# Two passes instead of three for the column scores of an attention loop, the shift row's transfer on two DMA queues, and another order of a turn

## The chip, the core and the metric

The kernel runs on one core of one Trainium2 chip. The metric is the device time of one launch, in microseconds, lower is better. The core has five engines that run side by side, each with its own instruction stream in order: TensorE (PE), VectorE (DVE), ScalarE (ACT), GpSimd (POOL) and SyncE (SP). They are kept in step by semaphores. DMAs are issued here by SP and by ScalarE, each on a queue of its own.

## The reference

A small language model's layer on 32 sequences of 128 tokens: token embedding with a windowed feature, one attention block with 16 heads, and a gated mixture of 16 experts. What the change touches is the attention:

```python
q = einsum('bsd,dhk->bshk', x, Wq) + bq
k = einsum('bsd,dhk->bshk', x, Wk) + bk
v = einsum('bsd,dhk->bshk', x, Wv) + bv
scores = einsum('bqhk,bshk->bhqs', q, k) * scale      # scale = 1/sqrt(64)
attn = softmax(scores, axis=-1)
ctx = einsum('bqhk,bshk->bqhk', attn, v)
attn_out = einsum('bqhk,hkd->bqd', ctx, Wo) + bo
y = layernorm(x + attn_out) * gamma + beta
```

The vocabulary has only 28 entries, so every token is a short vector: a one-hot of 28, a windowed share of 28, and a few constant columns, 64 with padding (UD). Two normalisations turn into two factors per token, r1 and r2. The scores of a head are then u^T G u with a 64x64 matrix G per head.

## The kernel before

Three stages stand one behind the other. Stage 1 (the first 46 us) builds tables. Its `nb` holds the token vectors without the factors, 128 tokens on the partitions, `uf` the vectors times r12 = r1 r2. TensorE transposes `uf`, split in two float16 parts, into `ub[r, b, part, :]`: the vectors on 64 rows, tokens along the columns, in both halves of the partitions. `nk` is the float16 copy of `nb` that the values use, with the factors s1 and s12 in its last columns. `keep_going` issues matmuls whose result nobody uses.

Stage 2 is a loop over the 32 sequences, software-pipelined: turn i of the loop handles the scores of sequence i+4, its second half's row scores, the column scores of i+3 and i+2, the values of i+2 and i+1, the output of i+1 and the normalisation of i, all interleaved. Each engine has its own loop over i in STEPS and its own order, written out by hand. The chain for one sequence b, in halves hf of eight heads (names are the functions of the listing below):

- `q_rows` (TensorE) makes G u for four pairs of heads in bank A[hf]; `q_hi` (ScalarE) and `q_lo` (VectorE) split it in float16 parts `qh` and `ql`.
- `score_rows` (TensorE) computes rough scores with queries on the partitions; it writes both banks of A, so it waits for both `q_lo`. `maxima` (VectorE) takes the row maxima, `maxima_cols` (TensorE) transposes them, `max_row` (ScalarE) copies them negated to `mrow`, and SP moves this row by DMA into row SHIFT of `qh` in either half of the partitions, so that the next matmul subtracts the maximum on its own.
- `score_cols` (TensorE) computes the exact scores with keys on the partitions in the two banks ST, as three passes of 512 columns for each 64-row half: high part of u with `qh`, high with `ql`, low part with `qh`. The two halves of the partitions run side by side.
- `exps` and `probs_hi` (ScalarE) take the exponential and its float16 part, `probs_lo` (GpSimd) the rest. `exps(b, 2)` and `exps(b, 3)` read the banks ST that `score_cols(b+1, 0)` writes next, which waits for them; `exps(b, 0)` and `exps(b, 1)` stand the same way before `score_cols(b, 1)`.
- `values` and `turn` (TensorE), `sums`, `sum_root`, `context`, `context_lo` (VectorE) and `context_hi` (ScalarE) make the normalised context, `output` and `residual` (TensorE) the attention's output, `y_squares` (ScalarE), `var_y`, `root_y` (GpSimd) and `y_scaled` (VectorE) its normalisation; `h2`, `var_x`, `x_rows`, `x_cols`, `x_hi`, `x_lo` and `logits` prepare stage 3.

In the first turns, `token_rows` on ScalarE and VectorE fill the residual stream, and `log_rho` (VectorE) with two small exponentials on ScalarE prepares the bias of `exps`. Stage 3 (from about 345 us) is the mixture of experts and isn't touched.

The order of a turn before, on TensorE: residual(i), turn(i+1,0), values(i+1,1), logits(i-1), q_rows(i+4,0), score_cols(i+2,1), maxima_cols(i+3), turn(i+1,1), q_rows(i+4,1), output(i+1,0), values(i+2,0), score_rows(i+4,0), score_cols(i+3,0), x_cols(i), output(i+1,1), score_rows(i+4,1). A row of the trace names the line; in stage 2 these are L1212 `q_rows`, L1225 `score_rows`, L1238 `score_cols`, L1255 `values`, L1264 `turn`, L1273 `output`, L1278 `residual`, L1287 `x_cols`, L1309 `maxima_cols`; on ScalarE L944 `q_hi`, L953 `exps`, L959 `probs_hi`, L965 `context_hi`, L972 `max_row`; on VectorE L1053 `q_lo`, L1062 `maxima`, L1087 `context`, L1096 `context_lo`, L1103 `y_scaled`; on SP L836, the shift.

## Time and profile before

| | us |
|---|---|
| median of three runs | 538.77 (538.43 to 546.91) |
| the profiled execution | 537.01 |
| its span in the trace | 535.2 |
| TensorE busy | 497.3 (93%) |
| VectorE busy | 447.9 (84%) |
| GpSimd busy | 384.7 (72%) |
| ScalarE busy | 379.2 (71%) |
| granted TensorE clock, mean | 0.989 |

Busy means that an instruction of the engine was under way; issuing a DMA, waiting for a semaphore and branching don't count. "Idle before" is the time in which an engine did nothing before an instruction, with the instruction or DMA that ended it. The durations of matmuls overlap, as they are pipelined: the price of a group of matmuls is the distance from its start to the next group's start. ACTq and SPq are issues of DMAs on these engines' queues.

### The profile page before, as it was taken

What the parts mean: (1) busy time and instruction counts of PE and PEld (TensorE: products, weight loads), DVE (VectorE), ACT (ScalarE), POOL (GpSimd) and SP (SyncE); (2) the same over time, 40 slices, a digit from 0 to 9 for tenths busy, and PEclk for the clock granted to TensorE, in tenths of its full rate; (3) what the DMA queues carried; (4) which work ended last, traced back from release to release, by engine and by line L of the source; (5) the groups of instructions that cost most, each with busy time, mean ns of one, the idle gap of its engine ahead of it and who ended that gap; (6) DMA issues with size and microseconds to landing.
All of it is one profiled execution on the core that took longest, in us unless ns stands there. A gap on an engine that the chain in (4) does not pass through costs nothing. (4 is left out here: it accounts for less than half of the span.)

```text
span 535.2 us, 15239 instructions
## 1 busy us (share of the span) xinstructions
PE 497.3 (93%) x5567; PEld 362.8 (68%) x5567; DVE 447.9 (84%) x1054; ACT 379.2 (71%) x768; POOL 384.7 (72%) x519
## 2 busy tenths in 40 slices
PE   5988799999999999999999998769999999999984
PEld 3876567777777777776777775534466767777664
DVE  4797669999999999998999999868778898878675
ACT  2868778888898888988898887336766555556530
POOL 1025669888788888888888888750468798789783
PEclk9998989999999999999999999999999999999998
DMA  6800000000000000000000000000734163351011
GB/s 233 333 6 2 2 2 4 2 3 3 3 2 3 3 3 3 4 2 4 3 4 2 3 3 2 2 1 4 168 80 100 23 150 76 77 138 38 31 40 60
DMA packets 11902, 21.68 MB, mean 41 GB/s; under 512 B 4668, under 2 KB 9780, under 8 KB 10164
## 3 DMA queue, kind: packets, MB, share of 16 engines
q1 hardware_dynamic: 11410, 20.15, 13.8%
q8 instruction: 45, 0.74, 0.6%
q10 hardware_dynamic: 418, 0.55, 0.4%
q14 instruction: 29, 0.24, 0.2%
HBM read 16.24 MB, written 4.33 MB: 38 GB/s over the span
## 5 line engine op out<-in xcount | busy, mean ns | idle before, releaser
L845 POOL TENSOR_TENSOR s_pl<-s_pf,s_ph 128x512 f16<-128x512 f32 x128 | 147.0, 1160 | 8.7 <-ACT s_ph L959 8.7
L1062 DVE TENSOR_REDUCE s_mx<-ps 128x4 f32<-128x512 f32 x128 | 83.8, 677 | 17.6 <-PE ps L1225 14.1
L953 ACT ACTIVATE s_pf<-ps,s_ln_r 128x512 f32<-128x512 f32 x128 | 87.1, 683 | 11.4 <-PE ps L1238 8.9
L823 PE MATMUL ps<-s_xt_all,s_w1s 128*128 128x512 f16 x384 | 87.9, 379 | 2.2 <-ACT s_ub L1543 1.6
L1698 PE MATMUL ps<-s_w2s,s_hid 128*128 128x256 f16 x768 | 88.9, 273 | 0.0
L1698 PEld LDWEIGHTS ps<-s_w2s,s_hid 128*128 128x128 f16 x768 | 75.1, 98 | 11.0
L959 ACT ACTIVATE s_ph<-s_pf 128x512 f16<-128x512 f32 x128 | 74.0, 637 | 0.0
L1273 PE MATMUL ps<-s_zh,s_cth 128*128 128x256 f16 x256 | 69.9, 273 | 1.0 <-DVE s_ctl L1096 1.0
L1273 PE MATMUL ps<-s_zl,s_cth 128*128 128x256 f16 x256 | 69.8, 273 | 0.0
L1273 PE MATMUL ps<-s_zh,s_ctl 128*128 128x256 f16 x256 | 69.8, 273 | 0.0
L823 PEld LDWEIGHTS ps<-s_xt_all,s_w1s 128*128 128x128 f16 x384 | 37.3, 98 | 41.4 <-ACT s_ub L1543 2.1
L1238 PE MATMUL ps<-s_qh,s_ub 64*128 64x512 f16 x256 | 49.5, 383 | 1.1 <-DMA s_qh<-s_mrow 1.1
L1053 DVE SCALAR_TENSOR_TENSOR s_ql<-ps,s_qh 128x512 f16<-128x512 f32 x64 | 43.4, 679 | 7.4 <-ACT s_qh L944 7.1
L944 ACT ACTIVATE s_qh<-ps 128x512 f16<-128x512 f32 x64 | 38.2, 598 | 13.7 <-PE ps L1212 12.1
L1506 POOL TENSOR_TENSOR s_hid<-s_ub,s_hid 128x512 f16<-128x512 f32 x21 | 25.9, 1253 | 27.8 <-ACT s_hid L1550 27.6
L1096 DVE TENSOR_TENSOR s_ctl<-ps,s_cth 128x512 f16<-128x512 f32 x64 | 43.6, 681 | 0.1
L1087 DVE TENSOR_TENSOR s_cn<-ps,s_rsum 128x480 f32<-128x480 f32 x64 | 41.8, 653 | 1.2
L1212 PE MATMUL ps<-s_ub,s_gp 128*128 128x128 f16 x512 | 40.1, 224 | 1.7 <-PEq L218 1.6
L1264 PE MATMUL ps<-s_ident,s_cn 128*128 128x128 f32 x256 | 38.7, 273 | 2.4 <-DVE s_cn L1087 2.4
L965 ACT ACTIVATE s_cth<-ps 128x512 f16<-128x512 f32 x64 | 38.5, 602 | 2.7 <-PE ps L1264 2.7
L1255 PE MATMUL ps<-s_uh,s_ph 128*128 128x60 f16 x512 | 36.8, 190 | 0.2 <-issue 0.2
L1255 PEld LDWEIGHTS ps<-s_uh,s_ph 128*128 128x128 f16 x512 | 32.3, 97 | 6.9 <-issue 6.7
(246 smaller groups left out, 1149.0 us busy)
## 6 DMA issues: line engine op xcount, KB each, us to landing
s_rep<-picks SPq DMA_DIRECT2D x14, 512.0 KB, 6.7
s_stage<-in_w SPq DMA_DIRECT2D x2, 1024.0 KB, 14.3
out<-s_zh SPq DMA_DIRECT2D x16, 128.0 KB, 2.0
out<-s_lg SPq DMA_DIRECT2D x16, 128.0 KB, 1.7
s_stage<-in_wq SPq DMA_DIRECT2D x1, 1024.0 KB, 5.0
s_stage<-in_wk SPq DMA_DIRECT2D x1, 1024.0 KB, 6.7
s_stage<-in_wv SPq DMA_DIRECT2D x1, 1024.0 KB, 8.3
s_stage<-in_wo SPq DMA_DIRECT2D x1, 1024.0 KB, 10.8
```

Source lines behind the costliest of these rows:

```text
L823: mm = nc.tensor.matmul(hidden_bank(n)[:], w1s[:, wp, c, j * P:(j + 1) * P], xt_all[:, GB * g:GB * (g + 1), xp, c, :], start=(k == 0), sto ...
L845: nc.gpsimd.tensor_tensor(flat(pl[:, b % 2, 4 * j:4 * j + 4, :]), pf[:, j, :], flat(ph[:, b % 2, 4 * j:4 * j + 4, :]), ALU.subtract).then_ ...
L953: nc.scalar.activation(pf[:, j, :], ST[j % 2][:], ACT.Exp, bias=ln_r[:, b:b + 1]).then_inc(exp_done[j], 1)
L959: nc.scalar.activation(flat(ph[:, b % 2, 4 * j:4 * j + 4, :]), pf[:, j, :], ACT.Copy).then_inc(phi_done[j], 1)
L1053: nc.vector.scalar_tensor_tensor(out=flat(ql[:, b % 2, hf]), in0=A[hf][:], scalar=1.0 / G_SCALE, in1=flat(qh[:, b % 2, hf]), op0=ALU.mult, ...
L1062: nc.vector.tensor_reduce(mx[:, b % 2, c:c + 4], A[ab][:].rearrange("p (h k) -> p h k", h=4), AX.X, ALU.max).then_inc(max_done[hf][ab], 1)
L1087: nc.vector.tensor_tensor(cn[:, hf].rearrange("p t (a u) -> p (t a) u", u=UD)[:, :, 0:UV], CB[hf][:].rearrange("p (h u) -> p h u", u=UD)[: ...
L1096: nc.vector.tensor_tensor(flat(ctl[:, b % 2, 4 * hf:4 * hf + 4, :]), CB[hf][:], flat(cth[:, b % 2, 4 * hf:4 * hf + 4, :]), ALU.subtract).t ...
L1238: mm = nc.tensor.matmul(ST[ab][:], ub[r, b, part, :], flat(q[r, b % 2, hf]), start=(n == 0), stop=(n == 2))
L1255: mm = nc.tensor.matmul(CB[hf][:, c:c + UV], p[:, b % 2, h, :], nk[:, b, 0:UV], start=(n == 0), stop=(n == 1))
L1273: nc.tensor.matmul(YB[:, 0:D], c[:, b % 2, p, :], zz[:, p, :], start=(p == 0 and c is cth and zz is zh), stop=False)
L1698: mm = nc.tensor.matmul(zb[b % 4], hid[:, g % 2, hp, j, t * P:(t + 1) * P], w2s[:, wp, j, :], start=False, stop=(j == NJ - 1 and hp == 1))
```

## The change

Three things are done at once.

**Two passes.** The column scores no longer use `ub` (u times r12, two float16 parts) but `nkT`, the transposed token vectors without the factors, which need one float16 part. The passes are `nkT` with `qh` and `nkT` with `ql`. The factor r12 of the key comes in as the per-partition scale of the exponential. The factors of the constant rows (R2, ONE, SHIFT, each now two rows for a high and a low part) are written into `nkT` by DMA: `scale_rows` (TensorE) transposes four columns of `nk`, VectorE copies them to `srow`, and SP issues twelve row DMAs. `nkT` itself is made in stage 1: eight groups of eight matmuls on TensorE (some in place of filler), four copies on ScalarE, four on VectorE; ScalarE's copy from `nb` to `nk` stands later. `nkT` takes the memory of `ul`.

**The shift on two queues.** SHIFT has two rows in each half of the partitions, so the maxima's row goes out in four DMAs instead of two: two from SP for the lower half as before, two from ScalarE (`shift_rows`) for the upper half, behind `max_row` and `q_hi(i+4,0)` in ScalarE's order.

**The order of a turn.** TensorE: `score_rows(.,1)` moves from the end of a turn to behind the next turn's `residual`; `maxima_cols` ahead of `score_cols(i+2,1)`; `q_rows(.,1)` ahead of `turn(.,1)`. VectorE: both `q_lo` together at the top, `y_scaled` and the logits earlier, the first half's two maxima exchanged, `log_rho` earlier in the first turns. ScalarE: `probs_hi(.,0)` and `probs_hi(.,1)` from the end of a turn to the beginning of the next, around `context_hi(.,0)`; `max_row` ahead of `q_hi(.,0)`.

The diff, cut to its core:

```diff
-R2, ONE, SHIFT = 2 * V, 2 * V + 1, 2 * V + 2
-ONE_HI, UV = R2 + 2, R2 + 4
+R2, ONE, SHIFT = 2 * V, 2 * V + 2, 2 * V + 4
+UV = ONE + 2
...
-        u_top, u_rest, nk = uh[:, 0], ul[:, 0], uh[:, 1]
+        u_top, nk = uh[:, 0], uh[:, 1]
+        nkT = ul[:].rearrange("p a b u -> p (a b u)").rearrange("p (b t) -> p b t", t=P)
...
+                def nkt_cols(n):
+                    dve.wait_ge(nt_ready, 8 + n + 1)
+                    nc.vector.tensor_copy(nkT[:, 16 + 4 * n:20 + 4 * n, :].rearrange("p b t -> p (b t)"), NKT_BANKS[4 + n][:])\
+                        .then_inc(nkt_ok, 1)
+
+                nkt_cols(0)
+                nkt_cols(1)
...
+                def nkt_part(n):
+                    if 1 <= n < 4:
+                        pe.wait_ge(nt_ok, (1, 2, 4)[n - 1])
+                    elif n >= 4:
+                        pe.wait_ge(nt_ok, 4 + (2, 3, 1, 4)[n - 4])
+                    for k in range(4):
+                        for ab in range(2):
+                            mm = nc.tensor.matmul(NKT_BANKS[n][ab * UD:(ab + 1) * UD, k * P:(k + 1) * P], nb[:, 4 * n + k, :], ident16[:],
+                                                  start=True, stop=True)
+                    mm.then_inc(nt_ready, 1)
+
+                for n in range(4):
+                    nkt_part(n)
...
+                nkt_part(6)
+                nkt_part(7)
                 table(0, range(3))
+                pe.wait_ge(nkt_ok, 2)
...
+                sp.wait_ge(srow_step, 2)
+                for ab in range(2):
+                    for r, j in ((R2, 0), (R2 + 1, 1), (ONE, 2), (ONE + 1, 3), (SHIFT, 2), (SHIFT + 1, 3)):
+                        r += ab * UD
+                        sp.dma_start(nkT[r:r + 1, :, :], srow[:, j, :]).then_inc(in_srow, 16)
                 for b in range(B):
                     sp.wait_ge(mrow_done, b + 1)
-                    for ab in range(2):
-                        r = ab * UD + SHIFT
-                        sp.dma_start(qh[r:r + 1, b % 2].rearrange("o f t q -> o (f t) q"),
-                                     mrow[8 * ab:8 * ab + 8, b % 2, :]).then_inc(shift_in[b % 2], 16)
+                    for r in range(SHIFT, SHIFT + 2):
+                        sp.dma_start(qh[r:r + 1, b % 2].rearrange("o f t q -> o (f t) q"), mrow[0:8, b % 2, :])\
+                            .then_inc(shift_in[b % 2], 16)
...
-                    nc.scalar.activation(pf[:, j, :], ST[j % 2][:], ACT.Exp, bias=ln_r[:, b:b + 1]).then_inc(exp_done[j], 1)
+                    nc.scalar.activation(pf[:, j, :], ST[j % 2][:], ACT.Exp, bias=ln_r[:, b:b + 1], scale=r12[:, b:b + 1]).then_inc(exp_done[j], 1)
...
+                def shift_rows(b):
+                    act.wait_ge(mrow_done, b + 1)
+                    for r in range(UD + SHIFT, UD + SHIFT + 2):
+                        act.dma_start(qh[r:r + 1, b % 2].rearrange("o f t q -> o (f t) q"), mrow[8:16, b % 2, :])\
+                            .then_inc(shift_in[b % 2], 16)
...
+                    if has(i + 2) and i > -2:
+                        probs_hi(i + 2, 0)
                     if has(i + 1):
                         context_hi(i + 1, 0)
-                    if i == -3:
-                        max_row(0)
+                    if has(i + 2) and i > -2:
+                        probs_hi(i + 2, 1)
+                    if has(i + 3):
+                        max_row(i + 3)
                     if has(i + 4):
                         q_hi(i + 4, 0)
+                    if has(i + 3):
+                        shift_rows(i + 3)
                     if i == -3:
                         nc.scalar.preload_act_table(ACT.Exp)
                         act.wait_ge(ln_ok, 1)
                         nc.scalar.activation(rho_x[:], ln_0[:], ACT.Exp, scale=-1.0).then_inc(ln_ok, 1)
-                    elif has(i + 3):
-                        max_row(i + 3)
...
-                        probs_hi(i + 3, 1)
-                        probs_hi(i + 3, 0)
+                    if i == -3:
+                        probs_hi(0, 0)
+                        probs_hi(0, 1)
...
+                        q_lo(i + 5, 0)
                         q_lo(i + 5, 1)
-                    for n in DVE_TOKENS.get((i, 0), ()):
-                        token_rows(n)
+                    if i == -4:
+                        log_rho()
+                    elif i < -4:
+                        for n in DVE_TOKENS.get((i, 0), ()):
+                            token_rows(n)
                     if has(i + 2):
                         context_lo(i + 2, 1)
-                    if i == -4:
-                        log_rho()
                     if has(i + 3):
                         sums(i + 3, 0)
                     if has(i + 5):
-                        maxima(i + 5, 0, 0)
+                        maxima(i + 5, 0, 1)
                     if has(i + 3):
                         sum_root(i + 3, 0)
                     if has(i + 5):
-                        maxima(i + 5, 0, 1)
+                        maxima(i + 5, 0, 0)
...
+                    if has(i + 1) and i % 4 == 2:
+                        logits_out((i + 1) // 4)
                     for n in DVE_TOKENS.get((i, 2), ()):
                         token_rows(n)
                     if i in (27, 28, 29):
                         gate_part(dve, 2 * i - 53, early)
                     if has(i + 3):
                         sums(i + 3, 1)
-                    if has(i + 1) and i % 4 == 2:
-                        logits_out((i + 1) // 4)
+                    if has(i + 2):
+                        y_scaled(i + 2)
                     if has(i + 3):
                         sum_root(i + 3, 1)
                         context(i + 3, 1)
-                    if has(i + 2):
-                        y_scaled(i + 2)
-                    if has(i + 3):
                         context_lo(i + 3, 0)
-                    if has(i + 6):
-                        q_lo(i + 6, 0)
                     if has(i + 2):
                         x_sums(i + 2)
...
-                        pe.wait_ge(shift_in[b % 2], 32 * (b // 2) + 32)
+                        pe.wait_ge(shift_in[b % 2], 64 * (b // 2) + 64)
+                        if b == 0:
+                            pe.wait_ge(in_srow, 16 * 12)
                     for n in range(2):
                         if hf or b >= 1:
                             pe.wait_ge(exp_done[2 - 2 * hf + n], b + hf)
-                    for n, (part, q) in enumerate(((0, qh), (0, ql), (1, qh))):
+                    for n, q in enumerate((qh, ql)):
                         for ab in range(2):
                             r = slice(ab * UD, ab * UD + UD)
-                            mm = nc.tensor.matmul(ST[ab][:], ub[r, b, part, :], flat(q[r, b % 2, hf]),
-                                                  start=(n == 0), stop=(n == 2))
+                            mm = nc.tensor.matmul(ST[ab][:], nkT[r, b, :], flat(q[r, b % 2, hf]),
+                                                  start=(n == 0), stop=(n == 1))
...
+                def scale_rows():
+                    for j in range(4):
+                        mm = nc.tensor.matmul(MISC[0:B, j * P:(j + 1) * P], nk[:, :, R2 + j:R2 + j + 1].rearrange("p b o -> p (b o)"),
+                                              identh[:], start=True, stop=True)
+                    mm.then_inc(srow_step, 1)
...
+                scale_rows()
                 for i in STEPS:
                     if has(i):
                         residual(i)
+                    if has(i + 3):
+                        score_rows(i + 3, 1)
+                    tokens(i - 1, 2)
                     if has(i + 1):
                         turn(i + 1, 0)
                         values(i + 1, 1)
@@ -1338,14 +1402,14 @@
                         maxima_cols(0)
                     if has(i + 4):
                         q_rows(i + 4, 0)
+                    if has(i + 3) and i > -3:
+                        maxima_cols(i + 3)
                     if has(i + 2):
                         score_cols(i + 2, 1)
-                    if has(i + 3) and i > -3:
-                        maxima_cols(i + 3)
+                    if has(i + 4):
+                        q_rows(i + 4, 1)
                     if has(i + 1):
                         turn(i + 1, 1)
-                    if has(i + 4):
-                        q_rows(i + 4, 1)
                     tokens(i, 0)
                     keep_going(i, 3)
                     if has(i + 1):
@@ -1369,9 +1433,6 @@
                     if has(i + 1):
                         output(i + 1, 1)
                     keep_going(i, 1)
-                    if has(i + 4):
-                        score_rows(i + 4, 1)
-                    tokens(i, 2)
```

## Rows read from the trace of the kernel before

**Rows 1.** The page, part 1: busy us, share of the span and instructions.

```profile
PE 497.3 (93%) x5567; PEld 362.8 (68%) x5567; DVE 447.9 (84%) x1054; ACT 379.2 (71%) x768; POOL 384.7 (72%) x519
```

**Rows 2.** Timeline of ScalarE: start us, us, engine, line; `max_row` of sequences 2 and 31.

```profile
77.09 0.27 ACT L972 ACTIVATE s_mrow<-ps 16x128 f16<-16x128 f32 x1 [0.36 <-PE ps L1309]
...
324.73 0.27 ACT L972 ACTIVATE s_mrow<-ps 16x128 f16<-16x128 f32 x1 [0.87 <-PE ps L1309]
```

**Rows 3.** Timeline of TensorE: one wait for the shift row's DMA.

```profile
131.60 0.39 PE L1238 MATMUL ps<-s_qh,s_ub 64*128 64x512 f16 x2 [0.47 <-DMA s_qh<-s_mrow]
```

**Rows 4.** Timeline of TensorE, 204 to 213 us: starts of groups in one turn.

```profile
204.92 0.28 PE L1309 MATMUL ps<-s_ident,s_mx 128*16 128x128 f32 x1
...
207.88 0.40 PE L1225 MATMUL ps<-s_ub,s_qh 64*128 64x128 f16 x8
208.12 0.38 PE L1238 MATMUL ps<-s_qh,s_ub 64*128 64x512 f16 x2
208.33 0.38 PE L1238 MATMUL ps<-s_ql,s_ub 64*128 64x512 f16 x2
...
210.54 0.40 PE L1225 MATMUL ps<-s_ub,s_qh 64*128 64x128 f16 x8
210.87 0.39 PE L1278 MATMUL ps<-s_mr,s_ub 128*128 128x256 f16 x2
...
212.67 0.39 PE L1238 MATMUL ps<-s_qh,s_ub 64*128 64x512 f16 x2
```

**Rows 5.** Timeline of VectorE: second half's maxima, and the last `q_lo` behind them.

```profile
210.98 1.29 DVE L1062 TENSOR_REDUCE s_mx<-ps 128x4 f32<-128x512 f32 x2 [0.40 <-PE ps L1225]
...
215.34 0.67 DVE L1053 SCALAR_TENSOR_TENSOR s_ql<-ps,s_qh 128x512 f16<-128x512 f32 x1
```

**Rows 6.** Timeline of ScalarE in the same turn, max row to `exps(.,2)`.

```profile
205.24 0.27 ACT L972 ACTIVATE s_mrow<-ps 16x128 f16<-16x128 f32 x1 [0.36 <-PE ps L1309]
...
206.12 0.60 ACT L944 ACTIVATE s_qh<-ps 128x512 f16<-128x512 f32 x1
206.61 0.59 ACT L965 ACTIVATE s_cth<-ps 128x512 f16<-128x512 f32 x1
207.09 0.69 ACT L953 ACTIVATE s_pf<-ps,s_ln_r 128x512 f32<-128x512 f32 x1
```

**Rows 7.** Line 836, the shift's DMA issues on SP: duration ns min/median/max.

```profile
L836 SPq DMA_DIRECT2D s_qh<-s_mrow x64: 634/635/744, 56.2 to 325.7; - x64
```

**Rows 8.** Timeline of ScalarE at the start: a table load and its three DMA issues.

```profile
0.73 1.28 ACT L288 ACT_TABLE_LOAD   x1 [0.73 <-PEq L1757]
1.07 0.64 ACTq L290 DMA_DIRECT2D s_lhs_t<-in_embT  x1
1.75 0.69 ACTq L291 DMA_DIRECT2D s_fus_b<-in_fus_b  x1
3.81 0.37 ACTq L293 DMA_DIRECT2D s_fus_w<-in_fus_w  x1
```

**Rows 9.** Timeline of SP at the start: two of its issues.

```profile
1.18 0.42 SPq L222 DMA_DIRECT2D s_mask_i<-in_maskT  x1
...
5.32 0.24 SPq L232 DMA_DIRECT2D s_ex<-in_beta  x1
```

**Rows 10.** Timeline of ScalarE: `token_rows`, with a scale from a column.

```profile
49.04 1.57 ACT L983 ACTIVATE s_h<-ps,s_sig 128x256 f32<-128x256 f32 x4 [0.26 <-PE ps L1193]
```

**Rows 11.** Timeline of VectorE in stage 1: waits for the covariance and for `quads`.

```profile
18.58 0.29 DVE L446 TENSOR_TENSOR s_cres<-ps,s_cs 128x128 f32<-128x128 f32 x1 [1.90 <-ACT s_cs L306]
...
20.51 1.29 DVE L462 TENSOR_TENSOR s_h<-ps,s_nb 128x512 f32<-128x512 f32 x2 [0.18 <-PE ps L626]
```

**Rows 12.** Timeline of ScalarE: waits in stage 1, and before the first exponentials.

```profile
18.27 0.28 ACT L306 ACTIVATE s_cs<-ps 128x128 bf16<-128x128 f32 x1 [1.94 <-PE ps L599]
...
29.90 0.32 ACT L315 ACTIVATE s_q<-s_red,s_eps_x 128x32 f32<-128x32 f32 x1 [1.57 <-DVE s_red L466]
...
62.50 1.26 ACT L953 ACTIVATE s_pf<-ps,s_ln_r 128x512 f32<-128x512 f32 x2 [2.33 <-DVE s_ln_r L1069]
```

More of the change, by code:

```diff
@@ L200, in build @@
         UT_BANKS = [psum[n] for n in (2, 3, 6, 7)]
+        NKT_BANKS = [psum[n] for n in (1, 2, 3, 5, 2, 3, 1, 5)]
         TABLE_BANKS = [psum[4], psum[5], psum[4]]
@@ L264, in _ @@
                 pool.wait_ge(cleared, CLEARED["uf_0"])
-                nc.gpsimd.memset(uf[:, :, ONE:SHIFT + 1], 1.0).then_inc(cleared, 1)
-                pool.wait_ge(nt_ready, 4)
+                nc.gpsimd.memset(uf[:, :, ONE:ONE + 1], 1.0).then_inc(cleared, 1)
+                pool.wait_ge(nt_ready, 12)
                 nc.gpsimd.memset(nb[:, :, R2:R2 + 1], 1.0).then_inc(cleared, 1)
@@ L279, in _ @@
                 pool.wait_ge(nk_step, 3)
-                for n, src in ((R2, s1), (ONE_HI, s12)):
+                for n, src in ((R2, s1), (ONE, s12)):
                     nc.gpsimd.tensor_scalar(column(n), src[:], 1.0, 0.0, ALU.mult, ALU.add).then_inc(nk_step, 1)
                 pool.wait_ge(nk_step, 5)
-                for n, src in ((R2, s1), (ONE_HI, s12)):
+                for n, src in ((R2, s1), (ONE, s12)):
                     nc.gpsimd.tensor_tensor(column(n + 1), src[:], column(n), ALU.subtract)
@@ L302, in _ @@
                         .then_inc(nt_ok, 1)
-                act.wait_ge(n_ok, 2)
-                nc.scalar.activation(nk[:, :, 0:2 * V], nb[:, :, 0:2 * V], ACT.Copy)
+                for n in range(4):
+                    act.wait_ge(nt_ready, 4 + n + 1)
+                    nc.scalar.activation(nkT[:, 4 * n:4 * n + 4, :].rearrange("p b t -> p (b t)"), NKT_BANKS[n][:], ACT.Copy)\
+                        .then_inc(nt_ok, 1)
                 act.wait_ge(cs_ready, 1)
@@ L455, in _ @@
                                                op0=ALU.mult, op1=ALU.subtract).then_inc(mr_ok, 1)
+                nkt_cols(2)
+                nkt_cols(3)
                 def quads(g):
@@ L581, in _ @@
                         mm.then_inc(nt_ready, 1)
-                keep_going(15, psum[0][:, 0:FREE])
+                def nkt_part(n):
[8 more added lines that the diff above has]
+                    mm.then_inc(nt_ready, 1)
+                for n in range(4):
+                    nkt_part(n)
                 pe.wait_ge(in_id, 16)
@@ L590, in _ @@
                 tp.then_inc(mt_ready, 1)
-                keep_going(6, psum[0][:, 0:FREE])
+                nkt_part(4)
+                nkt_part(5)
                 pe.wait_ge(mt_ok, 1)
@@ L650, in gram @@
                 def gram():
-                    pe.wait_ge(qkv_ok, 4)
+                    pe.wait_ge(qkv_ok, 5)
                     for h in range(H):
@@ L662, in z_part @@
                         pe.wait_ge(wo_step, 2 * HD + 1)
-                        pe.wait_ge(qkv_ok, 7)
+                        pe.wait_ge(qkv_ok, 8)
                     elif n == 2:
@@ L680, in _ @@
                 quads(3)
+                pe.wait_ge(nkt_ok, 4)
                 table(1)
@@ L772, in build @@
         xc = sb2("xc", [P, 2, D])
+        srow = sb2("srow", [B, 4, P], F16)
         A, ST, CB, MISC, YB = psum[0:2], psum[2:4], psum[4:6], psum[6], psum[7]
@@ L1130, in token_rows @@
                             .then_inc(tok_done[n % 3], 1)
-                DVE_TOKENS = {(-5, 0): (2,), (-5, 1): (5,), (-5, 2): (8,), (-4, 0): (11,), (-4, 1): (13, 14)}
+                DVE_TOKENS = {(-5, 0): (2,), (-5, 1): (5,), (-5, 2): (8,), (-4, 1): (11,), (-4, 2): (13, 14)}
+                dve.wait_ge(srow_step, 1)
+                nc.vector.tensor_copy(srow[:].rearrange("b j t -> b (j t)"), MISC[0:B, :]).then_inc(srow_step, 1)
                 nc.vector.memset(cn[:].rearrange("p h t (a u) -> p (h t a) u", u=UD)[:, :, UV:UD], 0.0).then_inc(cn_zero, 1)
@@ L1300, in logits @@
                     mm.then_inc(lg_ready, 1)
+                def scale_rows():
[3 more added lines that the diff above has]
+                    mm.then_inc(srow_step, 1)
                 def maxima_cols(b):
+                    if b == 0:
+                        pe.wait_ge(srow_step, 2)
                     for n in range(2):
```

16 lines of the change are left out of this document (9 added, 7 removed).

## The prediction

> **What bounds the kernel now.** I read the page first: TensorE is busy 93% of the span, VectorE 84% [rows 1]. That is an average over three stages, and the change sits in the middle one, the loop over 32 sequences, so I read one turn of that loop from the timeline of each engine. The distance between two max rows gives the turn: from the one of sequence 2 (77.09) to that of sequence 31 (324.73) lie 29 turns in 247.64 us, 8.54 each [rows 2]. Most are 8.50; three are longer because TensorE waits for the shift row's DMA, once 0.47 [rows 3].
>
> TensorE issues without a visible hole through such a turn [rows 4]. One pass of `score_cols` over its 512 columns (both 64-row halves side by side) takes 208.12 to 208.33, 0.21, and there are six per turn. VectorE has one hole per turn, 0.40 before the second half's maxima [rows 5]. ScalarE waits 0.36 for the maxima's transposition [rows 6]. So TensorE is the bound, with VectorE 5% behind it, and SP's two DMA issues of 0.635 each [rows 7] stand on a queue that does nothing else.
>
> **What the change takes off TensorE.** Two passes of six: 2 x 0.21 = 0.43 a turn, 12.5 us in 29 turns. Everything below asks whether another chain lets the turn get that short. I set R as the start of `residual` and count from it.
>
> **Step 1, the new start of a turn.** `score_rows(.,1)` now stands behind `residual`. Old: `score_rows` 210.54, `residual` 210.87, second-half scores 212.67 [rows 4]. New: `residual` 0.23, about 0.09 for the change to 64 rows (`score_rows` takes 0.33 at 210.54, where `residual` with 128 rows follows, and 0.24 at 207.88, where 64 rows follow), then `score_rows` with its end 0.40 later. VectorE's maxima start 0.04 behind that end, as now (210.94, 210.98) [rows 4, 5], so at R+0.76; now they start at R+0.11. The transposition of the maxima comes behind `q_rows(.,0)`: 1.80 (210.87 to 212.67) + 0.33 + 0.09 - 0.10 = R+2.12.
>
> **Step 2, VectorE's chain.** From the maxima to the end of `q_lo(.,1)` the new order holds the same eleven instructions as the old one; old they take 210.98 to 215.34 + 0.67 = 5.03 [rows 5]. The scaled y now fills the reciprocal's wait, some 0.07 less. So `q_lo(.,1)` is done at 0.76 + 5.03 - 0.07 + 0.04 = R+5.76. `score_rows(.,0)` waits for it (207.88 to 208.12, 0.24), and then come the first-half scores, `x_cols` and `output(.,1)`: 208.12 to 210.54 is 2.42 now, less one pass 0.21, less 0.09 as `residual` needs no change of rows: 2.12 [rows 4]. Sum 5.76 + 0.24 + 2.12 = **8.12 us a turn**: VectorE alone would already keep back a little of the 0.43 (8.50 - 8.12 = 0.38).
>
> **Step 3, ScalarE's chain, the one that I think decides.** `shift_rows` puts two DMA issues on ScalarE's queue, of the shape that SP issues now in 0.635 each (634 to 744 ns over 64) [rows 7]. The page doesn't count issuing as busy, but the engine's queue is in order: `exps(.,3)`, `q_hi(.,1)`, `context_hi(.,1)` and `exps(.,2)` stand behind them, and `score_cols(.,0)` waits for `exps(.,2)`, since it writes the same banks. An issue can run beside the instruction before it: L290's runs from 1.07 within the table load of 0.73 to 2.01 [rows 8]. So `q_hi(.,0)` covers the start; nothing covers the rest. From R: transposition 2.12; max row 0.32 later (204.92 to 205.24) 2.44; its end +0.27, 2.71; two issues with a gap of 0.05 and 0.02 ahead, 4.05; `exps(.,3)` at about 4.10; + 0.57 (its 0.69 less the 0.11 by which `q_hi`'s 0.60 overlaps the next) 4.67; + 0.49 (206.12 to 206.61) 5.16; + 0.48 (206.61 to 207.09) 5.64 for `exps(.,2)`; + 0.69 + 0.04 = 6.37 for `score_cols(.,0)`; + 2.12 = **8.49 us a turn** [rows 4, 6, 7]. The old chain had `exps(.,2)` start at 207.09, 4.72 behind its `residual` one turn before 210.87, so the change pushes it 0.9 back, more than TensorE wins. ScalarE still has time for all of it: this is a chain, not its busy share.
>
> ScalarE's price per issue isn't known for this shape. From below, L293 took 0.37 on ScalarE, which gives 4.10 - 0.53 for `exps(.,3)` and 7.96 in this chain, so step 2's 8.12 holds. From above, L291 (one row of 1 KB) took 0.69 on ScalarE while SP issued too, and L232, the same size on SP, 0.24 [rows 8, 9]: 0.45 more. I take 0.66, between the loop row on SP and L291: 8.54 a turn. Against 8.54 now, the 29 turns give 0.
>
> The Trainium skill, DMA: Bandwidth & Descriptors, section Issuing engines are not separate DMA queues, says that issuing from several engines saves only sequencer time. By that rule splitting gains nothing in data movement; the trace agrees that the issue's 0.635 is what there is to place, and here it is placed on an engine with work behind it.
>
> **Step 4, the shift's landing.** Four DMAs instead of two, two on each queue, so the last is issued no later after the max row than now. There were 2.61 us between the max row's end (205.51) and the scores (208.12) [rows 4, 6]; new it is 6.37 - 2.71 = 3.66. So the three waits for it should go, 1.7 us less in all; I book half, -0.8 (rows 3 shows one).
>
> **Step 5, the rest.** The scale of `exps` as a column: `token_rows` has it, 0.39 for 256 columns [rows 10], against 0.60 for 512 without it [rows 6], on one line with a fixed part; 0. The transpositions of `nb` into `nkT` before the loop: 64 small matmuls; 48 take the place of filler, 16 are new right before the first table and `quads`. Eight of 128 columns cost about 0.5 (the span of `q_rows`, 1.80 less its neighbours), so `quads` comes some 1.1 later, and VectorE, which waited only 0.18 there and then works through [rows 11], comes later by that: +1.1. Four of their copies lie in VectorE's 1.90 and four in ScalarE's 1.94 of waiting in that stretch; the copy of `nb` to `nk` moves to where ScalarE waits 1.57 for VectorE [rows 11, 12]. Uncovered, each would be about 0.6 and 1.7. `scale_rows` +0.3. The twelve row DMAs on SP at 0.635 take 7.6 us from about 47.5 and end before the first shift (56.15) and the first scores (59.80); if that cover went, +2. Filling the loop: two issues ahead of the exponential's table load, +0.9, against `log_rho`, now ahead of the token rows: ScalarE waited 2.33 for it [rows 12]. I take -0.1 together, with 1.5 either way. Sum: 0 - 0.8 + 1.1 + 0.3 - 0.1 = +0.5; ScalarE at 0.69 instead of 0.66 would make it +2.2.
>
> **The rivals.**
> (a) *ScalarE's issues are cheap, under 0.45 each.* For it: L293's 0.37. Then step 2 rules: 8.12, 29 x -0.42 = -12.2, + 0.5 + 0.8 (the waits of step 4 count already): 538.8 - 10.9 = 528. If VectorE's chain is 0.15 shorter than I think, TensorE's own 7.94 (8.50 - 0.43 and the 0.12 by which `values` waits now) comes near: 522. Against it: the same shape costs 0.635 on SP, in all 64.
> (b) *The two queues get into each other's way.* SP and ScalarE wait for the same max row and issue in the same instant, each turn. For it: L291's extra 0.45. Against: SP's L222 ran from 1.18 to 1.60, 0.42, wholly inside L290's 1.07 to 1.71, so neither can have waited for all of the other [rows 8, 9]. If one issue of the two pays 0.45: 8.94 a turn, +11.6, 551. If both: 9.4, 564. It decides from 0.8 us per issue, where the kernel becomes more than 2% slower. The Trainium skill, Perfetto Trace Analysis, section DMA Instruction — HWDGE, says that an issue locks the descriptor generator for itself alone; taken fully, four issues in a row make 2.6 us instead of 1.3, 9.8 a turn, and about 575. The overlap of L222 and L290 speaks against the full form.
> (c) *The change doesn't shorten TensorE's turn at all, as the passes were hidden.* The trace has no hole beside them; 3%.
>
> **How the numbers follow.** Held by ScalarE at SP's price: 0.47, 535 to 546. (a): 0.23, 521 to 531. (b): 0.27, 549 to 575. (c) and the unknown: 0.03. The sum is made on the profiled execution, 537.0 with a span of 535.2, and the median of three is 538.8, 1.8 above it; I forecast on the median: 538.8 + 0.5, with the small losses of the fill rounded up, **540**. The range leaves out the ends of (a) and (b): 525 to 558. A measurement tells about 2% (528 to 549.6). Faster by more: most of (a)'s lower half and some of the rest, 0.2. Slower: (b) and a tail of the first, 0.3. Within: 0.5.
>
> **What would show it.** ScalarE's queue: the two issues, their length, and `exps(.,3)` right behind them, 1.0 after `q_hi(.,0)`. TensorE: a hole of about 0.5 before `score_cols(.,0)`, ended by ScalarE's exponential, and a turn of 8.5. In (a) the hole stands before `score_rows(.,0)`, ended by `q_lo`, and is under 0.2. In (b) the issues are 0.8 or longer on one of the queues. The forecast is wrong if ScalarE goes on to `exps(.,3)` without waiting for its own issues, or if the issue costs under 0.5.

## The result, and the profile after

The changed kernel takes **548.33 us** (median of four runs, 547.2 to 550.7) against 538.78 for the kernel before on the same chip: a ratio of 1.019, interval 1.016 to 1.023. The medians lie 9.6 us apart; of the two profiled executions, on which the readings below rest, the spans are 547.3 and 535.2, 12.1 apart. The granted TensorE clock was 0.994 over the span against 0.989 before, and 1.00 from 80 to 310 us in both executions, so the loop's part of the loss isn't the clock. In the turns that fill the loop it isn't the same: the kernel before was granted 0.62 and 0.53 from 66 to 70 us, the changed one 1.00. The time lies inside the range that was given. The forecast of 540 missed about 8 us.

Part 1 of the page after, to be held against [rows 1]:

```profile
PE 493.2 (90%) x5486; PEld 360.8 (66%) x5486; DVE 450.6 (82%) x1059; ACT 390.0 (71%) x773; POOL 386.6 (71%) x519
```

TensorE has 4 us less to do and its share fell from 93% to 90%: it works less and waits more. ScalarE is busy 11 us longer. Where the time went is read from the length of a turn, as in [rows 2], with the max rows of sequences 2 and 31 (timeline of ScalarE, start and duration in us):

```profile
74.31 0.25 ACT L1010 ACTIVATE s_mrow<-ps 16x128 f16<-16x128 f32 x1
...
335.87 0.27 ACT L1010 ACTIVATE s_mrow<-ps 16x128 f16<-16x128 f32 x1 [0.18 <-PE ps L1369]
```

The 29 turns take 261.56 us, **9.02 each**, where they took 247.64 and 8.54: +13.9. The fill came out shorter: the max rows of sequences 0 and 1 stand at 55.84 and 66.26, that of sequence 2 at 74.31 instead of 77.09, -2.8. What follows the last max row takes 211.4 instead of 210.5, +1.0, whose cause no reading here shows. The sum is +12.1, the whole difference.

Now one turn, of 9.02 us. It is one of those in which the two issues took 1.49 together; in most they took 1.40, and the commonest turn is 8.93. Timeline of ScalarE, which answers to [rows 6]; ACTq is its queue's DMA issuing. `residual` starts on TensorE at 233.75, so R = 233.75:

```profile
236.22 0.27 ACT L1010 ACTIVATE s_mrow<-ps 16x128 f16<-16x128 f32 x1
236.40 0.57 ACT L982 ACTIVATE s_qh<-ps 128x512 f16<-128x512 f32 x1
236.52 1.49 ACTq L1015 DMA_DIRECT2D s_qh<-s_mrow  x2
238.12 0.78 ACT L991 ACTIVATE s_pf<-ps,s_ln_r,s_r 128x512 f32<-128x512 f32 x1 [1.15 <-issue]
238.80 0.59 ACT L982 ACTIVATE s_qh<-ps 128x512 f16<-128x512 f32 x1
239.28 0.60 ACT L1003 ACTIVATE s_cth<-ps 128x512 f16<-128x512 f32 x1
239.75 0.79 ACT L991 ACTIVATE s_pf<-ps,s_ln_r,s_r 128x512 f32<-128x512 f32 x1
```

Behind `q_hi(.,0)` (236.40 to 236.97) the engine does nothing for 1.15 us; "issue" as the releaser says that it waited for no other engine. It is its own queue: both issues, 1.49 us together, stand ahead of `exps(.,3)`. Then the same turn on VectorE, and on TensorE, which answers to [rows 4]; the brackets hold the wait ahead of an instruction and what ended it:

```profile
239.42 0.69 DVE L1102 SCALAR_TENSOR_TENSOR s_ql<-ps,s_qh 128x512 f16<-128x512 f32 x1 [0.62 <-ACT s_qh L982]
```

```profile
233.75 0.38 PE L1330 MATMUL ps<-s_mr,s_ub 128*128 128x256 f16 x2
...
235.91 0.27 PE L1369 MATMUL ps<-s_ident,s_mx 128*16 128x128 f32 x1
...
240.26 0.40 PE L1275 MATMUL ps<-s_ub,s_qh 64*128 64x128 f16 x8 [0.62 <-DVE s_ql L1102]
240.64 0.39 PE L1290 MATMUL ps<-s_qh,s_ul 64*128 64x512 f16 x2
240.86 0.39 PE L1290 MATMUL ps<-s_ql,s_ul 64*128 64x512 f16 x2
...
242.77 0.38 PE L1330 MATMUL ps<-s_mr,s_ub 128*128 128x256 f16 x2
```

The hold passes from ScalarE's `q_hi(.,1)` to VectorE's `q_lo(.,1)` (0.62 late) and to TensorE's `score_rows(.,0)` (0.62 late). `score_cols(.,0)` starts at 240.64, 0.1 behind the end of `exps(.,2)` at 240.54, and 0.38 behind the start of `score_rows(.,0)`, where 0.24 was enough in the kernel before (207.88 to 208.12). So both branches of ScalarE's late chain arrive nearly together, and the exponential closes it, by 0.14. The list of waits, 120 to 320 us (line, releaser: us in total, times, longest), shows it in every one of the 22 turns, and not one wait for a DMA:

```profile
ACT s_pf L991 <- issue: 26.0, 23, 1.7
...
DVE s_ql L1102 <- ACT s_qh L982: 13.3, 22, 1.2
PE ps L1275 <- DVE s_ql L1102: 13.3, 22, 1.2
DVE s_mx L1111 <- PE ps L1275: 11.9, 22, 0.5
```

The list for TensorE's weight loads has one more wait, before `output`, to which experiment 6 comes back:

```profile
PEld ps L1325 <- DVE s_ctl L1145: 4.1, 23, 0.2
```

Last, the instructions by source line (ns, min/median/max): the exponential of after, the issues on SP and on ScalarE, and in a second fence the exponential of before.

```profile
L991 ACT ACTIVATE s_pf<-ps,s_ln_r,s_r x128: 770/791/813, 61.5 to 347.0; 128x512 f32<-128x512 f32 x128
L874 SPq DMA_DIRECT2D s_qh<-s_mrow x64: 625/629/694, 56.1 to 336.8; - x64
L1015 ACTq DMA_DIRECT2D s_qh<-s_mrow x64: 627/744/1420, 56.1 to 336.8; - x64
```

```profile
L953 ACT ACTIVATE s_pf<-ps,s_ln_r x128: 662/689/693, 62.5 to 335.0; 128x512 f32<-128x512 f32 x128
```

The same exponential takes 0.10 us longer since its scale comes from a column.

### The profile page after: what moved, and what is told of

It reads as the page before. It is cut to its first block and busy times, and to the rows that moved or that the text cites. A ratio compares the mean times of both kernels' runs of the same rounds, so it can differ in the third digit from the quotient of the medians.

```text
span 547.3 us, 15165 instructions
## 1 busy us (share of the span) xinstructions
PE 493.2 (90%) x5486; PEld 360.8 (66%) x5486; DVE 450.6 (82%) x1059; ACT 390.0 (71%) x773; POOL 386.6 (71%) x519
## 5 line engine op out<-in xcount | busy, mean ns | idle before, releaser
L991 ACT ACTIVATE s_pf<-ps,s_ln_r,s_r 128x512 f32<-128x512 f32 x128 | 101.0, 791 | 35.3 <-issue 35.0
L997 ACT ACTIVATE s_ph<-s_pf 128x512 f16<-128x512 f32 x128 | 76.9, 633 | 0.1
L1316 PE MATMUL ps<-s_ident,s_cn 128*128 128x128 f32 x256 | 41.7, 285 | 5.6 <-DVE s_cn L1136 5.6
L1275 PE MATMUL ps<-s_ub,s_qh 64*128 64x128 f16 x512 | 25.5, 217 | 20.0 <-DVE s_ql L1102 19.0
L1262 PE MATMUL ps<-s_ub,s_gp 128*128 128x128 f16 x512 | 38.9, 219 | 0.0
L982 ACT ACTIVATE s_qh<-ps 128x512 f16<-128x512 f32 x64 | 37.0, 580 | 1.4 <-PE ps L1262 1.4
L1262 PEld LDWEIGHTS ps<-s_ub,s_gp 128*128 128x128 f16 x512 | 29.1, 97 | 12.8 <-issue 12.7
```

What stands on the lines that cost most here:

```text
L991: nc.scalar.activation(pf[:, j, :], ST[j % 2][:], ACT.Exp, bias=ln_r[:, b:b + 1], scale=r12[:, b:b + 1]).then_inc(exp_done[j], 1)
L997: nc.scalar.activation(flat(ph[:, b % 2, 4 * j:4 * j + 4, :]), pf[:, j, :], ACT.Copy).then_inc(phi_done[j], 1)
L1262: mm = nc.tensor.matmul(A[hf][:, t * P:(t + 1) * P], gp[:, hf, t].rearrange("p a u -> p (a u)"), ub[:, b, part, :], start=(part == 0), sto ...
L1316: tp = nc.tensor.transpose(CB[hf][:, t * P:(t + 1) * P], cn[:, hf, t, :], ident[:])
```

## The experiments

The theory: **the two issues stand on ScalarE's in-order queue between the max row and the exponentials, and their 1.4 us, with the longer exponentials behind them, set the turn.** The rivals: the two queues get in each other's way; the longer exponential alone is the loss; the new order itself costs; the passes taken off TensorE were hidden. All ratios are to the kernel before, run beside each kernel; turns are the mean of the 29.

**1. The exponential without its scale.**

```
-  nc.scalar.activation(pf[:, j, :], ST[j % 2][:], ACT.Exp, bias=ln_r[:, b:b + 1], scale=r12[:, b:b + 1])
+  nc.scalar.activation(pf[:, j, :], ST[j % 2][:], ACT.Exp, bias=ln_r[:, b:b + 1])
```

> The changed kernel, with the column scale r12 left out of the exponential, so the probabilities are computed without that factor. In the changed kernel one such exponential takes 0.79 us instead of 0.69, four per turn, two of them on ScalarE's chain from the DMA issues to the first-half column scores. Theory A (that chain sets the turn, 9.02 us): exponentials 0.69 again, turn 8.78 to 8.82, time 541 to 543 us. Rival (the turn is set by the shift row's landing or by TensorE's order): the exponentials get shorter, the turn stays at 9.0, time 547 to 549.

543.52 us, ratio 1.012 (1.008 to 1.017), turn 8.72. The exponential is back near its old length:

```profile
L991 ACT ACTIVATE s_pf<-ps,s_ln_r x128: 680/701/727, 64.6 to 340.9; 128x512 f32<-128x512 f32 x128
```

The mean turn lost 0.30, more than the 0.2 of two exponentials between the issues and `score_cols(.,0)`, and the timelines say why: something else got shorter as well. In the commonest turn of each kernel (8.93 and 8.62) the two exponentials give 0.18, and 0.12 comes from the issue pair, which takes 1.28 here instead of 1.40, although SP still issues at the same instant (ScalarE, then SP):

```profile
243.28 1.28 ACTq L1015 DMA_DIRECT2D s_qh<-s_mrow  x2
```

```profile
243.27 1.31 SPq L874 DMA_DIRECT2D s_qh<-s_mrow  x2
```

So the column costs about 0.2 a turn, as the theory put on it, and why the pair got shorter isn't shown. 0.18 a turn over the kernel before stays: the column is a part and not the whole. The medians lie only 4.8 us apart, where 29 turns at 0.30 would be 8.7; in the profiled execution of this kernel the max row of sequence 2 comes 2.8 us later than in after (77.11 against 74.31), with a granted clock of 0.84 and 0.82 from 40 to 60 us against 1.00.

**2. All four issues on SP**, none on ScalarE (the second part of the edit is in ScalarE's order).

```
-for r in range(SHIFT, SHIFT + 2):
-    sp.dma_start(qh[r:r + 1, b % 2].rearrange("o f t q -> o (f t) q"), mrow[0:8, b % 2, :])\
+for ab in range(2):
+    for r in range(SHIFT, SHIFT + 2):
+        r += ab * UD
+        sp.dma_start(qh[r:r + 1, b % 2].rearrange("o f t q -> o (f t) q"), mrow[8 * ab:8 * ab + 8, b % 2, :])\
...
-if has(i + 3):
-    shift_rows(i + 3)
```

> The changed kernel, all four shift DMAs issued by SP, none by ScalarE: undoes the second queue alone. Theory A (the two issues on ScalarE cost 1.2 us of its chain): ScalarE has no hole before exps(.,3) any more; the last of four issues of 0.63 us ends 2.6 us behind the max row and lands up to 1.3 us later, so TensorE now waits up to that landing: turn 8.2 to 8.8, time 524 to 542 us, faster than the changed kernel in any case. Rival (the four transfers themselves or the new order cost the time, whoever issues them): 548 or more.

544.1 us, ratio 1.013 (1.006 to 1.020), turn 8.78: the turn as expected, the time 2 us above. ScalarE is free, and TensorE now waits for the landing instead. Waits of 120 to 320 us, and one of them from TensorE's timeline:

```profile
PE ps L1290 <- DMA s_qh<-s_mrow: 9.8, 23, 0.9
```

```profile
208.14 0.39 PE L1290 MATMUL ps<-s_qh,s_ul 64*128 64x512 f16 x2 [0.35 <-DMA s_qh<-s_mrow]
```

The max row ends at 204.31; the four issues stand on SP's queue for 2.67 us (204.33 to 207.00), and TensorE goes on at 208.14, so the last row has landed 3.8 behind the max row's end at the latest. So one queue is too little for four rows, and an engine with work behind it is too dear: the question is where on ScalarE's queue they stand.

**3 and 4. The issues moved behind other work of ScalarE.** In the third kernel the first issue stands behind `q_hi(i + 4, 0)`, where both stood, and the second behind `exps(i + 2, 3)`. In the fourth:

```
 q_hi(i + 4, 0)
-shift_rows(i + 3)
 exps(i + 2, 3)
+shift_row(i + 3, 0)
 q_hi(i + 4, 1)
+shift_row(i + 3, 1)
```

> The changed kernel, same DMAs on the same queues, but ScalarE issues one behind q_hi(.,0) and the other behind exps(.,3), so that each issue runs while an activation does. Theory A: exps(.,3) starts about 0.75 earlier in the turn, first-half column scores at R+6.2 instead of R+6.9: turn 8.3, time 526 to 530 us. Rival (an issue waits for the engine to be empty, or keeps the engine from running): turn stays near 9.0, 546 to 550 us.

> As e3_split, but the issues stand behind exps(.,3) and behind q_hi(.,1): both wholly beside an activation, but the second is issued about 0.4 later. Theory A: turn 8.15 to 8.3, then set by VectorE's chain (q_lo) or by the landing, time 523 to 529 us; if the landing takes more than 1.3 us behind the issue, TensorE waits for the DMA and it is slower than e3_split. Rival (issues block the engine wherever they stand): 546 to 550 us.

530.33 us, ratio 0.986 (0.980 to 0.993), turn 8.35; and 528.68, 0.985 (0.980 to 0.989), turn 8.24. Moving the second issue behind one exponential takes 18 us off, moving both takes 20. The fourth was measured again, with more runs:

> e4_late once more with more rounds, for its interval against the kernel before: ratio 0.980 to 0.987.

**524.47 us, ratio 0.975 (0.973 to 0.978)**, turn 8.28 (8.17, every fourth 8.32, and one of 9.31, in which TensorE waited 1.0 for the shift's DMA): faster than both kernels. The interval that was expected, 0.980 to 0.987, was missed. The ratios 0.985 and 0.975 are of one and the same kernel, and its times go with the granted clock of the execution: 527.3 to 530.2 us at 0.987 to 0.992 in the first set, 523.1 to 524.8 at 0.994 to 0.999 in the second, where the one execution at 0.988 took 528.3. Of the 2.7 us between the two profiled spans 2.6 lie ahead of the first max row (57.95 against 55.35), where the first had 0.88 to 0.95 and the second 1.00. What makes the chip grant the one or the other isn't shown. The kernel before ran at 0.99 in the median of both sets, so about 1% of the 2.5% may be the clock, and effects under 1% between sets aren't read here. One turn of it, ScalarE's timeline:

```profile
204.21 0.27 ACT L1010 ACTIVATE s_mrow<-ps 16x128 f16<-16x128 f32 x1
204.38 0.57 ACT L982 ACTIVATE s_qh<-ps 128x512 f16<-128x512 f32 x1
204.76 0.63 ACTq L1015 DMA_DIRECT2D s_qh<-s_mrow  x1
204.86 0.76 ACT L991 ACTIVATE s_pf<-ps,s_ln_r,s_r 128x512 f32<-128x512 f32 x1
205.51 0.63 ACTq L1015 DMA_DIRECT2D s_qh<-s_mrow  x1
205.52 0.57 ACT L982 ACTIVATE s_qh<-ps 128x512 f16<-128x512 f32 x1
...
206.74 0.77 ACT L991 ACTIVATE s_pf<-ps,s_ln_r,s_r 128x512 f32<-128x512 f32 x1
```

Each issue now runs while an activation ahead of it in the program computes: the first begins at 204.76, with `q_hi` still busy and `exps(.,3)` about to run to 205.62. `exps(.,2)` starts 2.53 behind the max row (236.22 to 239.75 in after: 3.53). One microsecond less on the chain, of which TensorE and VectorE let 0.85 through. And ScalarE's issue costs 0.63 here, not 0.74, although SP's two run beside it (by source line, then SP's timeline in the same turn):

```profile
L1015 ACTq DMA_DIRECT2D s_qh<-s_mrow x64: 627/627/1031, 55.6 to 313.6; - x64
```

```profile
204.50 1.31 SPq L874 DMA_DIRECT2D s_qh<-s_mrow  x2
```

**5. The two queues kept apart.** SP waits for `exps(.,3)` too before it issues, so that only ScalarE issues behind the max row.

```
 sp.wait_ge(mrow_done, b + 1)
+if b >= 1:
+    sp.wait_ge(exp_done[3], b)
```

> The changed kernel, SP holding its two shift issues back until exps(.,3) behind ScalarE's issues is done, so that ScalarE issues alone. Read here is the length of ScalarE's issue (median 0.744 beside SP's): if the two queues get into each other's way, it falls to 0.63, with exps(.,3) 0.15 to 0.25 earlier behind the max row; if 0.744 is ScalarE's own price, it stays. The turn itself gets longer, since SP's rows land later: 9.5 to 9.9 us.

570.62 us in one run, turn 9.64; SP's rows land later and TensorE waits for them, which was the price of the probe. Its reading is ScalarE's issue alone, and the wait behind the pair (timeline of ScalarE):

```profile
L1017 ACTq DMA_DIRECT2D s_qh<-s_mrow x64: 627/627/1083, 58.1 to 357.5; - x64
```

```profile
202.50 1.28 ACTq L1017 DMA_DIRECT2D s_qh<-s_mrow  x2
203.88 0.78 ACT L993 ACTIVATE s_pf<-ps,s_ln_r,s_r 128x512 f32<-128x512 f32 x1 [0.94 <-issue]
```

From the start of the issues to the exponential pass 1.38 us here and 1.60 in the turn of after shown above, 1.51 in its commonest turn. So what was expected came, and by itself it would say that the two queues get in each other's way. But experiments 1 and 4 speak against that reading: in both SP issues while ScalarE does, and ScalarE's issue has a median of 628 and 627 ns. What is left to it are some longer turns, about every fourth, in which the pair took 1.49 in after, 1.50 in experiment 1 and 1.31 here. SP's issues beside it aren't enough to make ScalarE's longer; what made them 1.40 a pair in the other turns of after isn't shown. The Trainium skill, Perfetto Trace Analysis, section DMA Instruction — HWDGE, has an issue wait for a lock on the descriptor generator. The rows show 0.1 to 0.2 us a pair, not the 0.63 that a full turn at the lock would cost.

**6. Is a pass of TensorE worth anything, and where?** A third pass over the columns was put back, in the second half's scores, and in another kernel in the first half's (`hf == 0`).

```
-for n, q in enumerate((qh, ql)):
+qs = (qh, ql, ql) if hf == 1 else (qh, ql)
+for n, q in enumerate(qs):
...
```

> The changed kernel, with a third pass (the low part of q once more, so that the sum is not the reference's) in the second half's column scores only. Theory A: these scores stand ahead of TensorE's wait of 0.6 us and beside ScalarE's two issues, off the chain: turn stays 9.02, 547 to 549 us, and the wait before score_rows(.,0) shrinks by 0.2. Rival (each pass off TensorE is time): 554 us, as with the pass in the first half.

> The changed kernel, with a third pass (the low part of q once more, so that the sum is not the reference's) in the first half's column scores only. Theory A: this pass stands on the closing chain, behind exps(.,2): turn 9.02 + 0.21 = 9.23, 554 to 555 us. Rival (TensorE stands idle 0.6 us a turn, so that a pass costs nothing): 548.

Second half: 547.61 us, ratio 1.019 (1.015 to 1.022), turn 9.03, no different from after. First half: 555.07, 1.033 (1.027 to 1.040), turn 9.20. The pass costs its 0.2 only behind the hole. Ahead of it the pass is taken up by waits, but not by the one that I named: the wait before `score_rows(.,0)` goes down by 0.05 a turn only (13.3 us in 22 turns to 12.2), and the rest goes into the wait before `output`, 4.1 us in 23 in after, which is gone from this kernel's list.

```profile
PE ps L1275 <- DVE s_ql L1102: 12.2, 22, 1.1
```

So of the 0.43 taken off TensorE half was worth nothing in this kernel as it stands.

**7. The new order alone**, on the kernel before: its three passes and SP's two issues stay, only the order of the turn on TensorE, ScalarE and VectorE is the new one.

> The kernel before (three passes, two DMAs a turn, both on SP, ub for the column scores, no scale), with the changed kernel's order of a turn on TensorE, ScalarE and VectorE. One part of the change alone. Theory A: nothing is on ScalarE's queue, so VectorE's chain from the turn's start sets it: q_lo done at R+5.7, + 0.24 + 0.2 + 2.33 = 8.4 to 8.5 a turn against 8.54, and the filling turns win 2.8 us as they did in the changed kernel: 530 to 536 us, faster than before by 0.5 to 1.5%. Rival (the new order costs by itself): 540 or more.

533.24 us, ratio 0.990 (0.983 to 0.996), turn 8.49 (8.44 and 8.58, one of 9.28). The order is no loss; it brings a little. The loss is in the rest: the issues and the scale.

**8. Late issues without the scale.**

> e4_late (both issues beside activations) without the column scale r12 in the exponential, so the probabilities lack that factor. Theory A: in e4_late the chains through VectorE and through GpSimd set the turn, not ScalarE's, so the 0.1 us per exponential no longer costs anything: turn 8.17, time within 0.3% of e4_late. Rival (ScalarE is nearly full and its busy time counts): 8.05 or less, 524 us.

524.53 us, ratio 0.978 (0.974 to 0.982), turn 8.23 (8.17 and 8.32). The steady turns are those of the fourth kernel to the hundredth: the same 0.10 per exponential that was worth about 0.2 a turn in after is worth nothing once ScalarE isn't the chain. This settles that the scale hurts by where it stands, and that no more is to be had from it.

**9 and 10. What holds the best kernel.** The theory was VectorE's chain from `score_rows(.,1)`, so that went ahead of `residual`; the rival, which I held for likelier, was a hole before the scaled y.

```
-if has(i):
-    residual(i)
 if has(i + 3):
     score_rows(i + 3, 1)
+if has(i):
+    residual(i)
```

> e4_late, with TensorE's score_rows(.,1) ahead of residual instead of behind it, so that VectorE's maxima start 0.3 earlier. Theory A (the chain from score_rows through the maxima to q_lo sets the turn of 8.17 in e4_late, and nothing else is near): turn 7.95 to 8.05, 521 to 524 us. Rival B: residual now ends 0.33 later, the root of its variance comes at 2.15 behind the turn's start, and the scaled y, which stands early in VectorE's order, waits for it: VectorE gets a hole of about 0.4 before L1156 (y_scaled), turn 8.15 to 8.3, 526 to 530 us. I hold B for likelier.

534.41 us, ratio 0.993 (0.990 to 0.996), turn 8.47, against 8.17 to 8.32: it went the wrong way, and both turns forecast (7.95 to 8.05, and 8.15 to 8.3 for the rival) missed. The rival's hole of about 0.4 is there; VectorE waits for GpSimd:

```profile
202.90 0.48 DVE L1154 SCALAR_TENSOR_TENSOR s_ytmp<-ps,s_ry,s_ga_b 128x256 f32<-128x256 f32 x1 [0.37 <-POOL s_ry L897]
```

So in the next kernel the scaled y went behind `context(i + 3, 1)` as well, out of the root's way.

> e8_late_early, with the scaled y back behind the second half's context on VectorE, where the kernel before had it. If rival B of e8_late_early holds, the hole before the scaled y is gone: turn 7.95 to 8.05, near TensorE's own 7.95, 520 to 524 us. If not, this changes nothing against e8_late_early.

535.76 us, ratio 0.998 (0.994 to 1.001), turn 8.48, where 7.95 to 8.05 was expected if the hole was all. The wait moved two instructions on (VectorE, then TensorE):

```profile
212.38 0.43 DVE L1160 BATCH_NORM_STATS2 s_bsx<-s_h 128x6 f32<-128x256 f32 x1 [0.27 <-POOL s_h L904]
```

```profile
214.35 0.40 PE L1278 MATMUL ps<-s_ub,s_qh 64*128 64x128 f16 x8 [0.20 <-DVE s_ql L1104]
```

A chain that I hadn't in my sum starts at `residual`: the squares on ScalarE, the root and the sum on GpSimd, the sums and `q_lo` on VectorE, then `score_rows(.,0)`. That the two chains end about together with `residual` first is my reading of the three kernels. What exactly is the floor under the 8.17 of the best kernel isn't shown; no run took `residual`'s chain alone.

## Why the prediction was right and wrong, step by step

**The mechanism of step 3 was the right one.** ScalarE goes on to `exps(.,3)` only behind its own issues, the chain runs as written, and moving the issues (experiments 3 and 4) removes it. Its terms, in us from R, against the turn shown above. The forecast column is the sum at SP's 0.635 an issue; with the 0.66 that I took it ends at 8.54:

| step | forecast | measured |
|---|---|---|
| maxima's transposition | 2.12 | 2.16 |
| max row | 2.44 | 2.47 |
| the issues start | 2.73 | 2.77 |
| `exps(.,3)` | 4.10 | 4.37 |
| `q_hi(.,1)` | 4.67 | 5.05 |
| `context_hi(.,1)` | 5.16 | 5.53 |
| `exps(.,2)` | 5.64 | 6.00 |
| `score_cols(.,0)` | 6.37 | 6.89 |
| next `residual` | 8.49 | 9.02 |

Up to the issues every term is right within 0.04, and from `score_cols` to the end of the turn 2.12 was right too (2.13). The 0.5 us between lies in three terms that were sized too small. Of the mean turn's 9.02, another tenth is in turns longer than the commonest, every fourth with the logits by 0.15, which the sum left out.

**The term that failed first is the 0 in step 5 for the scale of `exps` as a column.** I took it from `token_rows` [rows 10], a line of another function (a copy) and another width, whose fixed part I could only draw through, and booked nothing; the exponential went from 0.69 to 0.79, and two of them stand on the chain (from `exps(.,3)` to `q_hi(.,1)` 0.68 instead of 0.57, from `exps(.,2)` to `score_cols(.,0)` 0.89 instead of 0.73). Experiment 1 takes it out: the two steps are 0.59 and 0.80 there, so the column makes 0.18 a turn of their 0.27. The other 0.09 is in the same two steps without the column: I had made them of the exponential's 0.69 and the gaps of other rows, a little too short. Experiment 8 shows that off the chain the column costs nothing. The row that I cited had no exponential in it, and a bound from above was missing.

**The second is the issue pair in step 3**, 1.60 from its start to `exps(.,3)` in the turn shown and 1.51 in the commonest, instead of 1.37 (1.42 at 0.66 an issue). Experiment 5, with SP out of the way, gives 1.38 for the same distance, which is the sum's own number; but so does experiment 1, 1.38 to 1.39 in its commonest turn, with SP issuing at the same instant. So the surcharge is measured, 0.14 to 0.23, and rival (b), which I had given a chance of 0.27 and a price of 0.45, is borne out at most in those longer turns, as 0.2 a pair. By its bound of 0.8 us per issue it didn't decide (744 ns in the median; the sum itself passes 2% at 0.84).

**The place of the hole was one group off.** Forecast: about 0.5 before `score_cols(.,0)`, ended by the exponential. Measured: 0.62 before `score_rows(.,0)`, ended by `q_lo(.,1)`. That is where rival (a) put its sign, and read without its releaser it would have spoken for VectorE. I had followed ScalarE's chain through `exps(.,2)` only and not through `q_hi(.,1)`, which VectorE's last `q_lo` needs: 5.05 + 0.62 to that instruction, + 0.69, + 0.15 is 6.51 for `score_rows(.,0)`. Both branches hang on the same hold, and `exps(.,2)` still ended last, by 0.14, so the turn wasn't affected; the reading would have been.

**Step 2 held.** `q_lo(.,1)` done at R+5.76 and 8.12 a turn were the VectorE chain's; in the fourth kernel, where the issues are gone from the chain, it is done at R+5.65 (206.11 + 1.27 from R = 201.73) and the turn is 8.17. Every fourth is 8.32, as the logits come in, which the sum left out. Rival (a)'s time of 528 came to pass in that kernel (528.7 and 524.5): the gain was there, and the issues' place held it back.

**The step "what the change takes off TensorE"** was right in size (0.2 a pass in experiment 6) and right in that another chain decides. Half of it was worth nothing in this kernel: of rival (c), the passes hidden, that much was true, behind waits that TensorE has in the changed kernel.

**Step 4 held.** The three waits for the shift's DMA are gone. **Step 5**, the fill: `quads` starts 1.1 later as summed, and the root at the end of stage 1 waits for it (VectorE, then ScalarE, against [rows 11, 12]).

```profile
21.62 1.28 DVE L477 TENSOR_TENSOR s_h<-ps,s_nb 128x512 f32<-128x512 f32 x2
```

```profile
28.29 1.69 ACT L348 ACTIVATE s_uh<-s_nb 128x1792 f16<-128x1792 bf16 x1
31.00 0.32 ACT L319 ACTIVATE s_q<-s_red,s_eps_x 128x32 f32<-128x32 f32 x1 [1.03 <-DVE s_red L481]
```

The root comes at 31.00 instead of 29.90. The moved copy of 1.69 is covered, with 1.03 of waiting left behind it, and so are the twelve row DMAs (SP, from 48.54 to 56.09):

```profile
48.54 7.55 SPq L870 DMA_DIRECT2D s_ul<-s_srow  x12
```

But the first max row stands at 55.84, as before (55.88). The 1.1 is still there when ScalarE's work for stage 1 ends (47.03 against 45.93), and is won back in a stretch in which the kernel before was granted a clock of 0.50 and 0.65 (46 to 50 us) and the changed one 1.00. So that the two stand level is luck of these two executions in part, and how much isn't shown. Filling the loop brought 2.8 where I had -0.1 with 1.5 either way. 1.0 of it is there at the first exponential (61.47 against 62.50), to which `log_rho` ahead of the token rows belongs: it waited 2.33 [rows 12] and now 0.28:

```profile
61.47 1.45 ACT L991 ACTIVATE s_pf<-ps,s_ln_r,s_r 128x512 f32<-128x512 f32 x2 [0.28 <-PE ps L1290]
```

The rest comes by the second max row, where the kernel before had 0.62 and 0.53 of the clock, and where the order and the passes changed too; these aren't told apart.

In all: the loop +13.9 where -0.8 was booked, the fill and prologue -2.8 where +1.3 was, the tail +1.0 where nothing was. Terms of one chain that were half a microsecond too small in each of 29 turns are the miss, and that the forecast time still lay only 8 us off owes something to the fill, which erred the other way.

## What to carry to other kernels

A DMA issue is work of the engine that issues it: put it behind an instruction whose successors nobody waits for, or one long enough to cover it, not between a value and its users; here the same two issues, moved behind the next two activations, turned +1.9% into -1.5% and -2.5% in two sets of runs. Price an operand form that the trace doesn't show (a column where a constant stood) from both sides, above all where the instruction stands on the chain twice a turn. When a hold on one engine is found, follow every instruction behind it to its readers, as the hole can show up under another engine's name.

## What the runs showed of the hardware

The exponential of 128x512 from PSUM to SBUF with its bias from a column took 689 ns, and 791 with its scale from a column as well (701 with the scale taken away in the changed kernel). An issue of 2 KB from SBUF to SBUF took 629 to 635 ns on SP. On ScalarE it took 627 in the median with SP's issues later (experiment 5), and also with SP's running beside it (628 in experiment 1, 627 in the fourth kernel), but 744 in the changed kernel; what makes the difference isn't shown. An issue starts while the activations ahead of it in the program still compute (at 204.76 and 205.51 in the turn of the fourth kernel), so each of the two was covered by its own, while two in a row left the engine idle for 1.15 us.
